# Bias products on 96 rows, and numerators behind the next sums, in the linear attention of a six-layer kernel

## The reference

```python
q = heads(x @ Wq.T + bq)
k = heads(x @ Wk.T + bk)
v = heads(x @ Wv.T + bv)
g = jax.nn.sigmoid(heads(x @ Wg.T + bg))
q = jax.nn.elu(apply_rope(q)) + 1.0
k = jax.nn.elu(apply_rope(k)) + 1.0
...
S = S + jnp.einsum('bhtd,bhte->bhde', ki, vi)
Z = Z + ki.sum(axis=2)
num = jnp.einsum('bhtd,bhde->bhte', qi, S)
den = jnp.einsum('bhtd,bhd->bht', qi, Z)[..., None] + 1e-06
return ((S, Z), gi * num / den)
...
return out @ Wo.T + bo
...
x = _layernorm(x + _L1_attn_ref(x, L1_attn_Wq, L1_attn_bq, ...), axis=-1)
```

## Time and profile before

| | before |
|---|---|
| median of 3 runs | 1009.85 us |
| lowest and highest | 1009.58 and 1013.3 us |
| the profiled execution | 1009.48 us, span 1007.7 us |
| mean granted clock of PE | 0.994 |
| busy share of PE, DVE, ACT, POOL | 96%, 64%, 44%, 31% |
| share of the chain that ended last: PE, DVE, issue, ACT, POOL | 87%, 7%, 2%, 1%, 1% |

### The profile page before, as it was taken

The page is one execution under the profiler, slowest core; times in us unless marked ns, Lnnn a source line. Parts: engine busy times, 40 slices in busy tenths (PEclk is TensorE's granted clock), DMA queues, the critical chain, the costliest instruction groups (busy, mean ns, idle before and its releaser), DMA issues.

```text
span 1007.7 us, 18735 instructions
## 1 busy us (share of the span) xinstructions
PE 963.4 (96%) x6131; PEld 757.6 (75%) x6131; DVE 642.2 (64%) x1466; ACT 444.5 (44%) x870; POOL 312.0 (31%) x514
## 2 busy tenths in 40 slices
PE   7999999999999999999999989998999998999994
PEld 5788886688888888888887745567787775888883
DVE  3776777656555555555557567768777865555555
ACT  4777786422233222323222333325777784333331
POOL 1133123344444444444445130110000106344430
PEclk9999999999999999999999999999999999999998
DMA  8000000255433333333332000011111120554401
GB/s 282 19 17 18 2 2 1 65 169 179 144 127 115 110 112 110 116 110 110 110 113 88 0 10 1 1 34 38 30 33 36 34 67 21 126 154 109 111 20 42
DMA packets 37356, 75.20 MB, mean 75 GB/s; under 512 B 7116, under 2 KB 18360, under 8 KB 37154
## 3 DMA queue, kind: packets, MB, share of 16 engines
q1 hardware_dynamic: 37006, 74.18, 25.5%
q0 software_dynamic: 288, 0.23, 0.2%
HBM read 67.21 MB, written 2.40 MB: 69 GB/s over the span
## 4 chain that ended last, share of the span: by engine, by line
PE 87%; DVE 7%; issue 2%; ACT 1%; POOL 1%; DMA 0%; SPq 0%; POOLq 0%; DVEq 0%; ACTq 0%
PE ps L1053 34%; PE ps L1079 17%; PE ps L424 5%; PE ps L674 3%; PE ps L519 3%; PE ps L431 3%; PE ps L913 2%; PE ps L511 2%; PE ps L550 2%; PE ps L791 1%; PE ps L846 1%; PE ps L841 1%; DVE ps L1748 1%; PE ps L810 1%; PE ps L888 1%
## 5 line engine op out<-in xcount | busy, mean ns | idle before, releaser
L1053 PE MATMUL ps<-shared 128*128 128x512 f32 x1560 | 377.8, 391 | 1.2 <-POOL shared L2096 0.7
L1053 PEld LDWEIGHTS ps<-shared 128*128 128x128 f32 x1560 | 292.9, 188 | 65.4 <-issue 4.9
L1489 ACT ACTIVATE shared<-pT 128x512 fp32r<-128x512 f32 x130 | 82.2, 632 | 286.5 <-DVE pT L1909 286.5
L2109 POOL CAST shared<-wraw 128x512 fp32r<-128x512 f32 (+1 forms) x130 | 92.2, 709 | 293.1 <-PE ps L1079 279.5
L1912 DVE TENSOR_TENSOR al<-pT,shared 128x512 fp32r<-128x512 f32 x130 | 118.8, 914 | 90.8 <-ACT shared L1489 90.8
L1901 DVE TENSOR_TENSOR e<-e,ps 128x512 f32<-128x512 f32 x130 | 89.3, 687 | 122.1 <-PE ps L1053 117.8
L1079 PE MATMUL ps<-shared 128*128 128x512 f32 x520 | 160.3, 389 | 0.4 <-DVE al L1912 0.4
L2111 POOL TENSOR_TENSOR shared<-wraw,shared 128x512 fp32r<-128x512 f32 (+1 forms) x130 | 132.1, 1017 | 10.4
L1079 PEld LDWEIGHTS ps<-shared 128*128 128x128 f32 x520 | 97.5, 188 | 21.4 <-DVE al L1912 1.3
L1483 ACT ACTIVATE e<-ps 128x512 f32<-128x512 f32 x130 | 77.7, 597 | 73.4 <-PE ps L1053 73.4
L1909 DVE TENSOR_TENSOR pT<-e,kbd 128x512 f32<-128x512 f32 x130 | 99.9, 769 | 7.1
(11 more groups left out here) (230 smaller groups left out, 1397.8 us busy)
## 6 DMA issues: line engine op xcount, KB each, us to landing
kbd<-combine_C SPq DMA_DIRECT2D x46, 512.0 KB
wraw<-in_C_w SPq DMA_DIRECT2D x48, 384.0 KB, 8.6
kbd<-combine_F SPq DMA_DIRECT2D x15, 512.0 KB
wraw<-in_F_w SPq DMA_DIRECT2D x17, 384.0 KB, 6.9
kbd<-kbd SPq DMA_DIRECT2D x96, 32.0 KB, 1.9
kT<-kbd SPq DMA_DIRECT2D x48, 32.0 KB, 1.8
c_ctx_t<-in_ctx_t SPq DMA_DIRECT2D x1, 1024.0 KB, 9.1
out<-c_x_rows SPq DMA_DIRECT2D x2, 512.0 KB, 3.0
```

Source lines behind the costliest of these rows:

```text
L1053: mm = pe.matmul(GU[t][s], w[u][:, (c * 2 + s) * P:(c * 2 + s + 1) * P], xx[:, c, t * HALF:(t + 1) * HALF], start=(i == 0), stop=(i == 5))
L1489: act.activation(ah[t][:, :], a2[t], ACT.Copy).then_inc(S("ah"), 1)
L2109: pool.tensor_copy(wh[u][:, lo:hi], wraw[k][:, lo:hi]).then_inc(S("m_wh"), 1)
```

## The change

- The array of bias rows has 96 rows in place of 33; the rows added hold zeros against ones, so the sums are the same.
- `project` and `linear_project` use these 96 rows. `linear_project` no longer adds X on PE; `linear_residual` on DVE adds it while reading bank 6 and then calls `dve_stats`; ACT's `linear_z` is gone.
- PE's turn: project(t), linear_x_T(t-5), linear_out_T(t-3), sums(t-1), numerators(t-2), linear_project(t-3). Within `sums` the part on 128 rows comes first. `numerators` waits for `D_an` first, and for batches 0 and 1 three filler products stand ahead of it.
- ACT's turn: gates(t), linear_out_T(t-3), linear_x(t-5), features(t-1), exponentials(t). The gates are Tanh of half the argument (the sigmoid is (1 + tanh(x/2)) / 2), and `gates(b)` waits for the third step of `linear_out(b - 2)` in place of the second.
- DVE's turn: linear_features(t-1), linear_residual(t-4), rotary(t), linear_masks(t-1), linear_out(t-2), normalized(t-4). `linear_out` takes the reciprocal of the doubled 16 denominators, multiplies it with (1 + tanh), and that with the numerators.

The diff, cut to its core:

```diff
@@ shapes
-        braw = arena[0:33, filled["DE"]:filled["DE"] + 5 * D + P]
+        braw = arena[0:96, filled["DE"]:filled["DE"] + 5 * D + P]
@@ PE
-                    pe.matmul(ps[:, n, :], ones33[:, :], brow[:, n * HALF:(n + 1) * HALF], start=True, stop=False)
+                    pe.matmul(ps[:, n, :], ones96[:, :], brow[:, n * HALF:(n + 1) * HALF], start=True, stop=False)
...
-                for n, rows in enumerate((P // 2, P)):
+                for n, rows in ((1, P), (0, P // 2)):
...
             def numerators(b):
+                if b > 0:
+                    pe.wait_ge(S("D_an"), b)
+                if b < 2:
+                    pe_keep_pace(pe, 5, 3)
                 pe.wait_ge(S("D_qf"), b + 1)
                 pe.wait_ge(S("D_gm"), b + 1)
-                if b > 0:
-                    pe.wait_ge(S("D_an"), b)
...
-                pe.matmul(y_, ones33[:, :], brow[:, 2 * HALF:], start=True, stop=False)
-                pe.matmul(y_, ident[:, :], X[:, b, :], start=False, stop=False)
+                pe.matmul(y_, ones96[:, :], brow[:, 2 * HALF:], start=True, stop=False)
...
             for t in range(B + 1):
-                if at(t - 2) is not None:
-                    numerators(t - 2)
-                if at(t - 5) is not None:
-                    linear_x_T(t - 5)
-                if at(t - 3) is not None:
-                    linear_out_T(t - 3)
                 if at(t) is not None:
                     project(t)
...
+                if at(t - 5) is not None:
+                    linear_x_T(t - 5)
+                if at(t - 3) is not None:
+                    linear_out_T(t - 3)
                 if at(t - 1) is not None:
                     sums(t - 1)
+                if at(t - 2) is not None:
+                    numerators(t - 2)
@@ ACT
                 if b >= 2:
-                    act.wait_ge(S("D_div"), 3 * (b - 2) + 2)
+                    act.wait_ge(S("D_div"), 3 * (b - 2) + 3)
                     act.wait_ge(S("D_gmps"), b - 1)
-                act.activation(eg[b % 2][:, :], ps[:, 1, 0:D], ACT.Exp, scale=-1.0).then_inc(S("D_eg"), 1)
+                act.activation(eg[b % 2][:, :], ps[:, 1, 0:D], ACT.Tanh, scale=0.5).then_inc(S("D_eg"), 1)
...
             for t in range(B + 1):
-                if at(t - 4) is not None:
-                    linear_z(t - 4)
-                if at(t - 3) is not None:
-                    linear_out_T(t - 3)
-                if at(t - 5) is not None:
-                    linear_x(t - 5)
                 if at(t) is not None:
                     gates(t)
...
+                if at(t - 3) is not None:
+                    linear_out_T(t - 3)
+                if at(t - 5) is not None:
+                    linear_x(t - 5)
                 if at(t - 1) is not None:
                     features(t - 1)
@@ DVE
-                dve.tensor_scalar(den2, num[:, :, :, DH0], 1e-6, None, ALU.add).then_inc(S("D_div"), 1)
+                dve.tensor_scalar(den2, num[:, :, :, DH0], 1e-6, 2.0, ALU.add, ALU.mult).then_inc(S("D_div"), 1)
                 dve.wait_ge(S("D_div"), 3 * b + 1)
+                dve.reciprocal(dinv[:, :], den[:, :]).then_inc(S("D_div"), 1)
+                dve.wait_ge(S("D_div"), 3 * b + 2)
                 dve.wait_ge(S("D_eg"), b + 1)
-                dve.scalar_tensor_tensor(d2[:, :].rearrange("p (h w) -> p h w", w=DH0),
+                dve.scalar_tensor_tensor(r2[:, :].rearrange("p (h w) -> p h w", w=DH0),
                                          eg[b % 2][:, :].rearrange("p (h w) -> p h w", w=DH0), 1.0,
-                                         bc(den[:, :], 2, DH0), ALU.add, ALU.mult).then_inc(S("D_div"), 1)
-                dve.wait_ge(S("D_div"), 3 * b + 2)
-                dve.reciprocal(r2[:, :], d2[:, :]).then_inc(S("D_div"), 1)
+                                         bc(dinv[:, :], 2, DH0), ALU.add, ALU.mult).then_inc(S("D_div"), 1)
...
+            def linear_residual(b):
+
+                dve.wait_ge(S("y"), nb("D", b + 1))
+                dve.tensor_tensor(z[b % 2][:, :], ps[:, 6, 0:D], X[:, b, :], ALU.add).then_inc(S("z"), 1)
+                dve_stats(dve, "D", b, b % 2)
...
                 if at(t - 4) is not None:
-                    dve_stats(dve, "D", t - 4, t % 2)
-                if at(t - 2) is not None:
-                    linear_out(t - 2)
+                    linear_residual(t - 4)
                 if at(t) is not None:
                     rotary(t)
...
                 if at(t - 1) is not None:
                     linear_masks(t - 1)
+                if at(t - 2) is not None:
+                    linear_out(t - 2)
                 if at(t - 4) is not None:
                     normalized("D", t - 4)
```

More of the change, by code:

```diff
@@ L162, in build @@
         gm = oT[:, 0, :].rearrange("p (n c k) -> p n c k", n=2, c=C)
-        rows33 = shared[2][0:33, 0:5 * D + P]
-        brow = shared[2][0:33, 0:5 * D]
-        ones33 = shared[2][0:33, 5 * D:5 * D + P]
+        rows96 = shared[2][0:96, 0:5 * D + P]
+        brow = shared[2][0:96, 0:5 * D]
+        ones96 = shared[2][0:96, 5 * D:5 * D + P]
         den = sb("den", [P, 16])
-        d2 = sb("d2", [P, D])
+        dinv = sb("dinv", [P, 16])
         r2 = sb("r2", [P, D])
@@ L1287, in linear_out_T @@
                    .then_inc(S("D_at"), 1)
[L1289 to L1294, removed]
             def linear_x(b):
@@ L1400, in act_linear_cross @@
                 ep, es, ev, ef, el = (at(t - B - n) for n in range(5))
-                if t == B + 1:
-                    linear_z(t - 4)
                 for k in range(STEPS):
@@ L1421, in act_linear_cross @@
                         masks(es, k + 1)
-                    if k == 3 and do is not None:
-                        linear_z(do)
                     if k == 3 and ep is not None:
@@ L1677, in linear_out @@
                 num = ps[:, 4:6, 0:D].rearrange("p r (m w) -> p r m w", w=VW)
-                two = [x[:, :].rearrange("p (r m w) -> p r m w", r=2, w=DH0) for x in (eg[b % 2], d2, r2, an)]
+                two = [x[:, :].rearrange("p (r m w) -> p r m w", r=2, w=DH0) for x in (r2, an)]
                 den2 = den[:, :].rearrange("p (r m) -> p r m", r=2)
-                dve.tensor_scalar(den2, num[:, :, :, DH0], 1e-6, None, ALU.add).then_inc(S("D_div"), 1)
+                dve.tensor_scalar(den2, num[:, :, :, DH0], 1e-6, 2.0, ALU.add, ALU.mult).then_inc(S("D_div"), 1)
                 dve.wait_ge(S("D_div"), 3 * b + 1)
+                dve.reciprocal(dinv[:, :], den[:, :]).then_inc(S("D_div"), 1)
+                dve.wait_ge(S("D_div"), 3 * b + 2)
                 dve.wait_ge(S("D_eg"), b + 1)
-                dve.scalar_tensor_tensor(d2[:, :].rearrange("p (h w) -> p h w", w=DH0),
+                dve.scalar_tensor_tensor(r2[:, :].rearrange("p (h w) -> p h w", w=DH0),
                                          eg[b % 2][:, :].rearrange("p (h w) -> p h w", w=DH0), 1.0,
-                                         bc(den[:, :], 2, DH0), ALU.add, ALU.mult).then_inc(S("D_div"), 1)
-                dve.wait_ge(S("D_div"), 3 * b + 2)
-                dve.reciprocal(r2[:, :], d2[:, :]).then_inc(S("D_div"), 1)
+                                         bc(dinv[:, :], 2, DH0), ALU.add, ALU.mult).then_inc(S("D_div"), 1)
                 dve.wait_ge(S("D_div"), 3 * b + 3)
@@ L1690, in linear_out @@
                     dve.wait_ge(S("D_atr"), b)
-                dve.tensor_tensor(two[3], num[:, :, :, 0:DH0], two[2], ALU.mult).then_inc(S("D_an"), 1)
+                dve.tensor_tensor(two[1], num[:, :, :, 0:DH0], two[0], ALU.mult).then_inc(S("D_an"), 1)
+            def linear_residual(b):
+                dve.wait_ge(S("y"), nb("D", b + 1))
+                dve.tensor_tensor(z[b % 2][:, :], ps[:, 6, 0:D], X[:, b, :], ALU.add).then_inc(S("z"), 1)
+                dve_stats(dve, "D", b, b % 2)
             def residual(b):
@@ L1813, in dve_linear_cross @@
                     if k == 4 and do is not None:
-                        dve_stats(dve, "D", do, do % 2)
+                        linear_residual(do)
                     if k == 4 and ep is not None:
@@ L2086, in pool_biases @@
             loaded(pool, "D")
-            pool.tensor_copy(rows33, braw[:, :]).then_inc(S("brow"), 1)
+            pool.tensor_copy(rows96, braw[:, :]).then_inc(S("brow"), 1)
             pool.wait_ge(S("brow"), 1)
@@ L2262 @@
     d["D_wo"] = chunks(n[p + "Wo"].T[turn])
-    d["D_brow"] = np.zeros((33, 5 * D + P), np.float32)
+    d["D_brow"] = np.zeros((96, 5 * D + P), np.float32)
     d["D_brow"][:, 5 * D:] = 1
```

## The result

The changed kernel takes 1024.27 us (median; 1022.01 to 1028.37), the one before, beside it on the same chip, 1011.4 us. The ratio is 1.0129, with a 95% interval of 1.0098 to 1.0159. The forecast was 1016.5 us with a range up to 1023: the direction holds, the size doesn't, and the time lies just above the range. The profiled execution took 1028.37 us with a span of 1026.5, so 18.9 us more than the one of before. It was the slowest of the four executions; by the medians the change costs 12.9 us.

A forecast was written before the change was run, and what follows sets the result against it. PE's work list bounds the 9.06 us linear-attention turn. Savings against the gates' buffer wait net +3.3 us on 1009.85, giving 1013.1; clock falls add 3.4, giving 1016.5 us, own range 1014.5 to 1023, overall 1006 to 1023.

The forecast's parts named there:

- The term for the clock: Linear attention: PE's clock falls after about two of six waits, 1.7 us each, 3.4 us; bounds none and six.
- their spans stay: Expert stages and cross attention: touched only where they begin, so their durations were put as unchanged.
- The wait itself: Linear attention, turns 3 to 7: gates(t) waits for linear_out(t-2) to free its buffer; PE idles 2.6 us each turn.
- 96 rows: Bias products: weight loads beside them become hidden, so `project` falls from 4.59 to 3.9 us.
- a sign of being wrong: In `project`: a bias product that still takes 0.42 us would show the forecast wrong.
- Residual on DVE: In `linear_project`: identity products leave PE, 0.54 us, and one open load, about 0.15 us; 1.80 falls to 1.12 us.
- Reciprocal: In `linear_out` on DVE: 16 elements a row in place of 256, 1.75 us becomes about 0.2 us.
- The rival with two loads a turn: ACT: Tanh and Exp need different tables, two loads of 1.28 us a turn, 7.7 us in all, 1021 us; chance 0.05.
- The entry to the cross attention: Start of cross attention: shorter reciprocal gives back 1.5 us, two residuals add 0.45 each, shorter `linear_project` gives 0.7: -1.3 us.

The follow-up runs named there:

- the kernel with the third buffer: The changed kernel with a third buffer for the gates, so gates(b) waits for linear_out(b - 3): 1002.58 us, ratio 0.9898.
- the fillers kernel: The changed kernel with filler products in PE's idle stretches, behind the numerators of turn 2 and ahead of linear_project in turns 3 to 7: 1018.71 us, ratio 1.0051.
- old order: The changed kernel with the earlier order of calls on PE, ACT and DVE, sums with 64 rows first, no fillers: 1007.0 us, ratio 0.9939.
- the one with the wide `dinv`: The changed kernel with dinv allocated 256 columns wide in place of 16, of which 16 are used: 1020.23 us, ratio 1.0072.
- the kernel before with the unused tile: The kernel before with an unused tile of 16 columns ahead of the router's tiles, moving everything behind it by 64 bytes a partition: 1017.43 us, ratio 1.0055.
- changed twice: The changed kernel in its first measurement, 1024.27 us, ratio 1.0129, and run again unmodified beside the follow-up kernels, 1025.12 us, ratio 1.0115.
- all repaired: The changed kernel with a third gates buffer, dinv allocated 256 columns wide, and no filler products in turns 2 and 3: 997.89 us, ratio 0.9854.

## Why the prediction was right and wrong

Two steps failed. The term for the clock was mis-sized: 3.4 us reckoned, 6.4 us by the medians and 8.3 us in the profiled pair. And the expert steps were put at nothing ("their spans stay"): they cost about 4.3 us, an estimate. The wait itself, the mechanism that the forecast stood on, was right. The two steps together, 3.0 and 4.3 us, are about the 7.8 us by which the median lies above the forecast.

- **96 rows.** Right: `project` fell by 0.60 us in the kernel with this alone (0.7 reckoned), `linear_project` from 1.80 to 1.61 (0.15 reckoned), and 0.17 us came on top between the transpose and the bias product. In the changed kernel `project` takes 4.08 us in turn 5, from 639.92 to 644.00. Its first bias product still takes 0.42 us from start to start there, which had been named as a sign of being wrong; the gain stands in the rows behind it, and the whole step is what counts. Rows 3, on products with 100 rows, were the right ones to go by.
- **Residual on DVE.** Right, a little more than reckoned: in the kernel with the third buffer `linear_project` takes 0.90 us, not 1.12.
- **Reciprocal.** 0.29 us from start to start in place of 0.21; Tanh as long as Exp. There is still one table load of 1.28 us in the stage, but it moved from the Tanh, which finds its table, to the first Exp at 600.95: `sums(0)` waits 0.34 us for it. In exchange the 1.30 us are gone that `project(1)` waited for v before (595.73), which the prediction took to stay: turns 0 and 1 gave back 3.4 us and not 3.0. The rival with two loads a turn is out.
- **The wait for the gates' buffer.** Right in place, cause and length: Tanh directly behind DVE's product, the `aT` copy as the operation that ends PE's wait, 2.73 to 2.74 us idle where 2.6 was reckoned, 2.54 in turn 2. Turn 5 took 10.15 us (10.2 reckoned), turn 2 9.45 (8.9; from the numerators at 611.50 to the next `project` 3.2 us in place of 2.9). Without the clock the stage was to be 4.1 us late; the fillers kernel gives 4.8, half a microsecond of it in turn 7, whose wait was longer (3.1 us).
- **The clock.** The term that was mis-sized. Two falls at 1.7 us each were reckoned, 3.4 us. The stage lost about 8.3 us in the profiled execution, and five of its six turns show it. Both factors were too small: four waits led to a fall, those of turns 2, 3, 6 and 7, and a fall cost over 2 us, more than the one of rows 9. Turn 3 alone lost 3.7 us (14.45 against 10.72 with fillers). That it was two of six was a guess between none and six, from one stretch that kept its clock with 1.5 us of idle time; such a stretch says nothing of 2.7 us, and by the old order not even that 1.5 us is safe. Which waits lead to a fall no run explains: the changed kernel had the same four twice, the one with the wide `dinv` those of turns 4, 5 and 7.
- **The expert stages, "touched only where they begin; their spans stay".** Wrong, and the term that is missing: 0.033 us in each of 130 pairs of steps, 4.3 us, from the address of `al`. No row of before shows it, but the diff does: a tile of another size stands ahead of others.
- **The entry to the cross attention.** 0.8 us were to come back on balance from turn 8 on (0.5 lost, 1.3 gained). From the first queries of layer E to the end, the fillers kernel takes 350.8 us and the kernel before with the unused tile, whose expert steps are equal, 352.5 (1011.9 - 659.4): 1.7 us came back.

The sum of the profiled execution's +18.9 us: the eight turns 13.1 (the wait with the rest 4.8, the clock 8.3), the expert steps of layer C 3.0 (from the first product of its loop to the last it takes 399.1 us in the kernel before, 402.1 in the one with the unused tile), 0.4 behind the turns, where what came back at the entry to layer E stands against the expert steps of layer F and the end of the last fall. The remaining 2.4 us lie at the entry to layer C, where the clock fell once between 180 and 190 us (0.69 on average, 1.00 before): the first full expert step begins at 193.13 in place of 190.75. The change has no edit there, though its tiles have moved. And that stretch is below 1.00 in four of the nine profiles built from the changed kernel (changed twice, old order, all repaired) and in none of the five built from the one before, so whether it is chance stays open.

## What to carry to other kernels

When a step moves past another in one engine's order, look for the buffers that it frees: here one wait constant changed from 2 to 3, but the read it waits for had moved from the head of the turn to its tail, and two buffers were one too few. An idle stretch on PE has a second price, the clock of the work behind it: here four of six waits of about 2.7 us cost some 2 us more each, and with 33-row products far more. One stretch that kept its clock is weak evidence; fillers in the wait, or a kernel without it, tell what the clock costs. And keep the addresses of hot tiles when a tile ahead of them changes its size, or at least read the durations in stages that should not have changed.

## What the runs showed of the hardware

- Between products on 128 rows, one on 33 rows leaves weight loads open that one on 96 rows doesn't: 4.59 against 3.99 us for `project` with its two bias products, and the load behind the bias product begins 0.42 us after its start in place of 0.08. The Trainium skill, "TensorEngine Tiling (Array Packing)" (Key Properties), says that a change of the tiling mode drains the engine. The trace agrees with that, but no run tells a drain from another reason for the late load.
- Moving `al` by 64 bytes a partition lengthened the products of L1079 by about 3 ns in 390, and the kernel by 0.4%. A move of 1024 bytes cost nothing.
- PE's clock held through idle stretches of 1.4 us in every turn from turn 3 on, but fell once behind one of 1.07 us (old order), and fell behind four of the six waits of 2.5 to 3.1 us. It came back within the next `project` where the bias products had 96 rows. With 33 it stayed at 1.2 GHz through both halves of it in turns 5 to 7, for 8.8 us of unbroken work each time, with turns of 17.1 us.
